# Wide key and value projections one place sooner, and the first rest of a weight piece ahead of the first maxima

## The reference

```
q = x @ Wq;  k = ctx @ Wk;  v = ctx @ Wv          # per layer
probs = softmax(q k^T * scale (+ column bias))     # per head, 128 x 128
x = x + (probs @ v) @ Wo (+ bo)
```

## Time and profile before

| | |
|---|---|
| median of 3 runs | 367.73 us (366.75 to 367.9) |
| profiled execution | 366.39 us, span 364.6 us |
| granted TensorE clock | 0.999 |
| PE busy | 351.5 us (96%) |
| ACT busy | 279.7 us (77%) |
| DVE busy | 248.7 us (68%) |
| POOL busy | 177.8 us (49%) |

### The profile page before, as it was taken

One profiled execution on the slowest core, in us unless ns is written; L12 is line 12 of the kernel. 1 busy time (PEld: TensorE's weight loads), 2 busy tenths in 40 slices (PEclk: granted clock), 3 DMA queues, 4 the chain that ended last, 5 costly groups with the idle time before them and its releaser, 6 DMA issues.

```text
span 364.6 us, 10489 instructions
## 1 busy us (share of the span) xinstructions
PE 351.5 (96%) x3533; PEld 304.9 (84%) x3533; DVE 248.7 (68%) x1383; ACT 279.7 (77%) x1176; POOL 177.8 (49%) x204
## 2 busy tenths in 40 slices
PE   8899999999999999999999999999999999988985
PEld 7677888899999998798778778888999899867864
DVE  4878858647446456677787777477465866688884
ACT  4999998657575576667999999888557666587893
POOL 4886545723233234455677664343333334366661
PEclk9999999999999999999999999999999999999999
DMA  7910600000000000000000000000000000000000
GB/s 238 408 63 2 234 1 2 2 3 2 1 2 2 3 0 3 2 1 2 3 8 16 9 4 2 3 2 2 2 3 2 3 0 3 2 1 2 3 9 22
DMA packets 4883, 9.71 MB, mean 27 GB/s; under 512 B 480, under 2 KB 3296, under 8 KB 4576
## 3 DMA queue, kind: packets, MB, share of 16 engines
q1 hardware_dynamic: 4544, 8.72, 6.7%
q10 hardware_dynamic: 288, 0.34, 0.4%
HBM read 8.53 MB, written 0.52 MB: 25 GB/s over the span
## 4 chain that ended last, share of the span: by engine, by line
PE 83%; ACT 8%; DVE 4%; DMA 2%; issue 1%; SPq 1%; DVEq 0%
PE pt_ps L852 15%; PE scores_ps L839 10%; PE v_ps L886 9%; PE v_ps L904 9%; PE q_ps L791 8%; ACT probs L476 6%; PE fill_ps L703 5%; PE fill_ps L704 5%; PE fill_ps L705 5%; PE v_ps L874 4%; PE scores_ps L822 3%; DVE probs L594 3%; PE scores_ps L703 3%; PE scores_ps L705 2%; PE scores_ps L704 2%; DMA v<-in_ctxT 2%
## 5 line engine op out<-in xcount | busy, mean ns | idle before, releaser
L476 ACT ACTIVATE probs<-probs,negmax 128x128 f32<-128x128 f32 x512 | 198.5, 391 | 58.2 <-DVE negmax L594 58.0
L382 POOL TENSOR_TENSOR probs<-probs,inv 128x512 f32<-128x512 f32 x127 | 137.5, 1083 | 172.1 <-DVE inv L601 171.8
L476 ACT ACTIVATION_READ_ACCUMULATOR probs<-probs,negmax 128x1 f32 x512 | 97.3, 190 | 0.0
L594 DVE CUSTOM_DVE_ANT_0 probs<-scores_ps,col_bias 128x128 f32<-128x128 f32 x256 | 58.1, 283 | 37.4 <-PE scores_ps L839 37.4
L852 PE MATMUL pt_ps<-smalls,probs 128*128 128x128 f32 x512 | 69.6, 278 | 1.2 <-DVE probsT L614 0.7
L852 PEld LDWEIGHTS pt_ps<-smalls,probs 128*128 128x128 f32 x512 | 55.7, 141 | 15.7 <-issue 13.9
L614 DVE COPY probsT<-pt_ps 128x512 f32<-128x512 f32 x96 | 62.7, 681 | 1.6 <-PE pt_ps L852 1.5
L594 DVE CUSTOM_DVE_ANT_0 probs<-scores_ps,no_bias,inv_rms 128x128 f32<-128x128 f32 x128 | 36.8, 344 | 11.3 <-PE scores_ps L822 11.2
L594 DVE DVE_READ_ACCUMULATOR2_ANT negmax<- 128x1 f32 x512 | 42.4, 83 | 0.0
L839 PE MATMUL scores_ps<-kT,qT 64*128 64x128 f32 x512 | 37.2, 285 | 0.0
L594 DVE CUSTOM_DVE_ANT_0 probs<-fill_ps,no_bias,inv_rms 128x128 f32<-128x128 f32 x128 | 36.4, 340 | 0.6 <-DVE col_bias L555 0.4
(11 more groups left out here) (133 smaller groups left out, 611.6 us busy)
## 6 DMA issues: line engine op xcount, KB each, us to landing
kT<-in_kv_w SPq DMA_DIRECT2D x6, 512.0 KB, 5.1
w_qo<-in_qo_w SPq DMA_DIRECT2D x2, 1024.0 KB, 8.1
v<-in_ctxT SPq DMA_DIRECT2D x4, 256.0 KB, 8.7
v<-in_kv_w SPq DMA_DIRECT2D x2, 512.0 KB, 10.4
outT<-x SPq DMA_DIRECT2D x8, 64.0 KB, 1.6
x<-in_xT SPq DMA_DIRECT2D x1, 384.0 KB, 7.7
oT<-in_narrow_kv ACTq DMA_DIRECT2D x1, 256.0 KB, 4.1
wn<-in_narrow_w SPq DMA_DIRECT2D x2, 64.0 KB, 5.0
```

What stands on the lines that cost most here:

```text
L382: nc.gpsimd.tensor_tensor(p4, p4, inv[:, o % 2, side, :].unsqueeze(2).broadcast_to([P, 4, S]), ALU.mult,).then_inc(probs_made[side], 1)
L476: last = nc.scalar.activation(e, e, ACT.Exp, scale=-1.0, bias=negmax[:, o % 2, side, q:q + 1], accum_out=rowsum[:, o % 2, side, q:q + 1])
L594: last = nc.vector.tensor_tensor_reduce(out=probs[:, o % PROBS_RING, side, cols], in0=banks[bank][:, cols], in1=bias, scale=scale, scalar= ...
```

## The change

Two edits. `FILLS` lists every wide fill from `k0.0` to `v0.3` and `k1.0` to `k1.3` one place sooner: `k0.0` joins half slot 0 (three fills there), `vn1` moves from half slot 4 to 3, and half slot 9 keeps one fill instead of two. From half slot 10 on nothing is changed. And DVE's `split_piece(0)`, which came after both maxima of half slot 0, is issued before half slot 0, right behind the rest of the first context part.

```diff
@@ FILLS
-    0: [("vn0", Q0), ("kn1.0", A0)], 1: [("k0.0", Q0)], 2: [("k0.1", A0), ("k0.2", A1)], 3: [("k0.3", Q0)],
-    4: [("vn1", A0), ("k1.0", A1)], 5: [("k1.1", Q0)], 6: [("bias", A0), ("k1.2", A1)], 7: [("k1.3", B0), ("v0.0", B1)],
-    8: [("v0.1", B0), ("v0.2", B1)], 9: [("v0.3", B0), ("v1.0", B1)], 10: [("kn0.3", B0), ("v1.1", B1)],
+    0: [("vn0", Q0), ("kn1.0", A0), ("k0.0", A1)], 1: [("k0.1", Q0)], 2: [("k0.2", A0), ("k0.3", A1)], 3: [("vn1", Q0)],
+    4: [("k1.0", A0), ("k1.1", A1)], 5: [("k1.2", Q0)], 6: [("bias", A0), ("k1.3", A1)], 7: [("v0.0", B0), ("v0.1", B1)],
+    8: [("v0.2", B0), ("v0.3", B1)], 9: [("v1.0", B0)], 10: [("kn0.3", B0), ("v1.1", B1)],
@@ DVE, half(n, h)
                     transposes_out(o - 2, 0)
                     if not scalar_copy(o - 2):
                         transposes_out(o - 2, 1)
-                if o == 0:
-                    split_piece(0)
                 if valid(o):
                     inverse_sums(o, 0)
@@ DVE, before the loop over the half slots
             nc.vector.tensor_tensor(c_lo[:, 0], c_in[0], c_hi[:, 0].bitcast(F32), ALU.subtract).then_inc(c_split, 1)
+            split_piece(0)
             for n, h in HALVES:
                 half(n, h)
```

## The result

The changed kernel takes 366.74 us (median of 20 executions, 366.03 to 367.48), the kernel before 367.16 (20, 366.51 to 368.06). The ratio is 0.9983, 95% interval 0.9975 to 0.9992; put on before's 367.16 that is 0.62 us less (0.29 to 0.92). It is a gain, smaller than the 0.3% that the prediction called measurable. The means of these twenty and twenty executions, 367.21 and 366.69, differ by 0.52 us. Of the distance from the forecast, 1.14 us (367.88 to 366.74), half was there before any change: the forecast stood on 367.73, the median of three executions of before, and all twenty have 367.16. A later comparison with twelve more executions gave 0.9987 (0.9974 to 0.9999). Five executions of all kernels together took 867 us or more and are left out everywhere.

A forecast was written before the change was run, and what follows sets the result against it. ACT and DVE were taken to bound the kernel up to 38.65 us, PE from there on. +0.75 + 0.48 + 0.33 - 1.41 = +0.15 us on 367.73 gave 367.88 us, range 366.9 to 369.0.

The forecast's parts named there:

- the base: Starting time of the forecast: 367.73 us, the median of the runs shown, 1.34 us above the profiled execution.
- the first maxima: DVE, kernel start: split of piece 0 and POOL's inverse root take turns, so the maxima begin at 10.50, +0.75 us.
- PE's idle places: PE, half slot 0: the larger first half slot is hidden because PE is idle there at several places; priced at nothing.
- The two parts: Up to 38.65 us the chain runs over ACT and DVE (head); from there PE is never idle (run).
- the fill that leaves the run: PE, half slot 9: one wide fill instead of two, so the run is shorter; -1.41 us.
- The exchange of vn1 and k1.0: ACT, end of half slot 4: copies k1.0 (0.48) instead of vn1 (0.15), ahead of exponentials the chain needs; +0.33 us.
- The copy of k0.0: ACT, start of half slot 1: the copy stands ahead of the exponentials and is not hidden; +0.48 us.
- is no gain: DVE, between the two octets: removing the split at 11.93 saves nothing, as the next reciprocal needs exponentials that end later.
- If DVE goes first: Kernel start: split ends at 10.0 or 10.08, then POOL's inverse root takes 0.42, so maxima again at about 10.5.
- The head in all: Everything before PE's run: first maxima +0.75, copy of k0.0 +0.48 and exchange +0.33, together +1.56 us.
- no blocking at the start: Rival, kernel start: DVE's split runs at once and POOL's inverse root is not held; -0.35 us, 367.4; chance 0.12.
- The checks that the prediction named: Wrong if first maxima start before 10.2 or after 11, shifts at 28.23 and 18.67 differ, or PE waits after 40.25.

The follow-up runs named there:

- split_first_only: Against the kernel before: only the split of piece 0 moved ahead of the first maxima, fills list unchanged; ratios 0.9998 and 1.0008 in two runs.
- fills_only: Against the kernel before: only the fills list shifted, the split of piece 0 left behind the two maxima of half slot 0; ratio 0.998.
- before_both_holes: The kernel before with 13 warm-up matmuls added in half slot 0 on PE, 7 ahead of kn1.0 and 6 behind it; 368.82 us, ratio 1.0038.
- before_no_warm: The kernel before without seven of its idle-filling warm-up matmuls, ahead of half slot 0's fills and around the first narrow queries; ratio 1.0008.
- before_again_b: The kernel before, unchanged, run once more for a further profile, the second of two; 367.81 us.
- before_again_a: The kernel before, unchanged, run once more for a further profile, the first of two; 367.24 us.
- before_filled: The kernel before with eight idle-filling warm-up matmuls (16 in the profile) added on PE behind kn1.0 in half slot 0; ratio 0.9995.

## Why the prediction was off, point by point

Between the forecast of 367.88 and the median of 366.74 lie 1.14 us. Half of it, 0.57, is the base (367.73 against 367.16); the other half is the change itself (+0.15 forecast, -0.42 between the medians; -0.52 to -0.66 between means). What failed in the change are two steps: the +0.75 for the first maxima, and the zero for PE's idle places.

- **The two parts, and the fill that leaves the run: right.** PE enters its run once, waits for nothing behind it, and the rest of the program is 1.3 to 1.5 us shorter: from the entry to the end of the span it is 324.46 to 324.56 us in all eight profiles with the new list of fills, and 325.87 to 325.95 in the three of before and that of `split_first_only`.
- **The exchange of vn1 and k1.0, +0.33: right.** 0.32 by the profiles, and gone when undone.
- **The copy of k0.0, +0.48: right in length, incomplete otherwise.** It took 0.47, but the moved split gave 0.10 back, which the prediction said "is no gain"; together 0.37. In the other direction it assumed that k0.0 is always ready. In the second profile ACT waited for it, and the price was 0.66; in `fills_only`, where k0.0 waits for the late split, it was 0.9 (11.00 to 15.52 against 3.62).
- **The first maxima, +0.75: mis-sized.** Counted from the end of the context's rest, the maxima are 0.28 us later in the five profiles where piece 0 is in time, and 1.0 later in the two where it lands late (0.60 on the clock of the changed kernel's first profile, whose rest ended 0.40 earlier). Over 16 executions the split alone costs 0.38 +- 0.15. The step that failed is "If DVE goes first: split to 10.0 or 10.08, then 0.42, again about 10.5": the inverse root does not wait for a second VectorE instruction, it ran into the split and ended in it. By the Trainium skill's page "SBUF — State Buffer", section "Who interferes with whom", POOL should have gone first; it had begun first, and the split was not held by it (1.21 against 1.19 us). The blocking is real for GpSimd's large tiles (2.02 instead of 1.03 for the keys) but did not show between this split and an inverse root of 128x1.
- **The head in all.** At full clock the changed kernel is 0.25 +- 0.18 us faster than before, where the sum said +0.15. So copy and maxima together cost some 0.8 us and not 1.23 (-0.25 + 1.41 - 0.33 = 0.83); its second profile, where piece 0 was in time, says 0.94 (0.28 + 0.66). It is near the rival "no blocking at the start", -0.35 us, whose mechanism is the one that the profiles show and to which the prediction gave 0.12.
- **The rest is a step that the sum priced at nothing:** "Hidden: PE's larger first half slot (PE is idle there at several places)". The idle places were no free room. In 46 of 113 executions of before TensorE's clock falls behind them, at a price of 1.0 us (367.95 against 366.95), on average 0.41. With k0.0 among them it fell in 0 of 32. In means: -0.25 - 0.41 = -0.66 us, against the +0.15 forecast. How the 0.66 divides into these two is no firmer than the cautions under the table; the counts do not depend on them.
- **The base.** "The median of the runs shown is 1.34 us above the profiled execution, so I put the same +0.15 on it" leaned on three executions, whose median happened to be 0.57 us above that of twenty. It also took the distance as one that the change leaves alone. In part it was an early start of the profiled execution, and in part, as the later series show for before in general, the fallen clock, which the change removes; the clocks of the three themselves are not listed.
- **The checks that the prediction named** (maxima between 10.2 and 11, the same shift at half slots 2 and 4, no wait behind the entry) were all met: 10.35, 0.96 and 0.97, none. The first was met by luck. The maxima were 0.60 late because DVE stood 0.54 us for a piece that landed late, not because the inverse root waited; with the 0.28 of the other profiles they would have begun near 10.0, outside the band. The forecast times were 0.15 us too late at the exponentials of 11.55 (11.7), and about 0.3 at 15.54 (15.85) and at the entry, 39.93 (40.25). One profile could not show what only part of the executions have.

Shown by experiments: the size of the exchange and of the leaving fill, the price of the split alone, and that how often the clock falls goes with the work that PE has in half slot 0 (more of it without any projection moved: 1 of 12; less of it in the changed kernel: 7 of 12). Argued only: why the inverse root passes beside the split, and what the end of `before_both_holes` waits for. Open: what decides whether the clock falls in a given execution (`before_no_warm` fell no more often than before), and what makes the start of the kernel vary by 0.8 us and more between executions; the landing of piece 0 and of the first loads is part of it.

## What to carry to other kernels

When a projection or a fill is moved, ask what the hole that it leaves or fills does to TensorE's clock: here filling a hole off the critical path was worth some 0.4 us on average, no less than all else that the change did. One profiled execution shows one start; list the mean granted clock of every execution, and if it comes in two groups, compare within a group and count the groups apart. And before a list of fills is shifted as a whole, look at which copy stands directly ahead of exponentials that the chain waits for: leaving a small one (vn1) in its place beat the change itself by 0.46 +- 0.32 us. Take the base of a forecast from as many executions as will be compared with it: the median of three was 0.57 us off here.

## What the runs showed of the hardware

- TensorE's granted clock went to 0.50 after three microseconds in which PE was busy for 0.35 to 0.57 of each, with no idle stretch longer than 0.92 us in the profile (`before_again_b`). The mean over the execution shows it: 0.995 instead of 0.998 or more.
- With the same busy shares in the same places (0.58, 0.36, 0.63 in the profile of before) it didn't fall, nor in `before_again_a` behind an idle stretch of 1.35 us. Whether it does is not fixed by the program.
- A VectorE subtract with two SBUF inputs and the end of GpSimd's inverse root on 128x1 ran beside each other without loss: 9.67 for 1.21 us (1.19 alone), and 9.16 for 1.01 us, which the inverse root takes at this place without the split too. GpSimd's 128x512 keys took 2.02 instead of 1.03 us beside the same kind of subtract.
- 26 matmuls more, in half slot 0, went with a program end 1.7 us later behind its last output and one more packet on the instruction queue; 16 more did not (`before_filled`).
